# Copying router logits out of PSUM one batch earlier on VectorE, in the opening stage of a two-layer attention and mixture-of-experts kernel

## The chip, the cores and the metric

One core of one Trainium2 chip runs the whole program. The metric is the device time of one execution in microseconds (us), the median of three runs. TensorE is PE in the rows (PEld is its weight load), VectorE is DVE, ScalarE is ACT, GpSimd is POOL, SyncE is SP.

## The reference, cut to what matters

The input x has 8 batches of 512 tokens with 256 features. Layer 0 begins with a layer norm and a small router; the rest of the model (a mixer with cumulative sums, 16 experts that each take 64 tokens of every batch, then attention and 8 experts in layer 1) follows from them and is not touched.

```python
x = L0_attn_x                                   # (8, 512, 256)
xn = _layernorm(x, axis=-1)
s = _L0_attn_ref(xn, ...)                       # mixer
router_logits = jax.nn.silu(xn @ router_w1) @ router_w2      # (8, 512, 16)
expert_probs = jax.nn.softmax(router_logits.transpose(0, 2, 1), axis=-1)
expert_weights, token_indices = jax.lax.top_k(expert_probs, 64)
...
x = x + s * silu(expert output)
```

## The kernel before

The program is a chain of stages, each a block in which every engine works through its own instruction list in order; semaphores tie the lists together, and a block ends when all lists have ended. The stage of this case is the first one after the constants, `layer0_norm`. It loops over the NB = 8 batches; one batch is a tile of 128 partitions with T = 4 tokens each (512 KB). The next stage, `choose_tokens`, ranks tokens on VectorE and needs the logits of all batches.

For batch n the work passes through the engines like this:

- SP loads `x[n]` (`load_x`, L206), two batches ahead at first; in its loop it issues `load_x(n + 2)`, then waits for `xn_done` of batch n and stores `xn` (L217). So `load_x(n + 3)` goes out behind the store of batch n. After the loop it loads `wout` (L218) and writes 8 tiles of zeros to `f` (L220).
- VectorE: `statistics(n)` is four `bn_stats` (L307), four `bn_aggr` (L311) and one add of epsilon (L313). GpSimd raises the result to the power -0.5 (L281). VectorE then does `normalised(n)`, four `tensor_scalar` (L321), the last of which increments `xn_done`.
- TensorE: `transpose_x(n)`, eight 128x128 transposes (L233), waits for `xn_done`. ScalarE copies them to SBUF (L267). `hidden(n)` is the product with router_w1 (L241), ScalarE applies silu (L272), and `logits(n)` is the small product with router_w2 (L249), which increments `lg_ps`.
- VectorE's `logits(n)` waits for `lg_ps` and copies the 128x64 logits from PSUM to `k.logits` (L326), which increments `lg_sb`.

TensorE's list is written in this order: in turn n of its loop it has transposes of batch n + 1, hidden of batch n, logits of batch n - 1:

```python
            for n in range(NB):
                if n + 1 < NB:
                    transpose_x(n + 1)
                hidden(n)
                if n:
                    logits(n - 1)
```

The two PSUM banks for logits are used in turn; TensorE's `logits(n)` waits until VectorE has copied batch n - 2.

VectorE's list in turn n has statistics of batch n + 1, normalised of batch n, and from n = 3 on the copy of batch n - 3; the last three copies stand behind the loop.

Of the kernel before, what the change touches and what calls it, by code (L numbers as in the profile page):

```python
# [14 lines left out]
NB, S, D = 8, 512, 256  # L15
# [32 lines left out]
def land(eng, k):  # L48


    eng.sem_inc(k.made, 1)
# [135 lines left out]
def layer0_norm(nc, R, k, m, x_b, xn_b, f_b, w):  # L187
# [12 lines left out]
    with nc.Block() as block:  # L200

        @block.sync
        def _(sp):
            def load_x(n):
                sp.wait_ge(x_in[n % 2], 16 * (n // 2))
                sp.dma_start(x[n][:], at(x_b, n)).then_inc(x_in[n % 2], 16)  # L206

            load_x(0)
            load_x(1)
            sp.dma_start(rw1[:], w["rw1"]).then_inc(r_in, 16)  # L210
            sp.dma_start(rw2[:], w["rw2"]).then_inc(r_in, 16)
            sp.dma_start(m.wqkv[:], w["wqkv"]).then_inc(m.w_in, 16)
            for n in range(NB):
                if n + 2 < NB:
                    load_x(n + 2)
                sp.wait_ge(xn_done, n + 1)
                sp.dma_start(at(xn_b, n), xn[n % 2][:]).then_inc(xn_out[n % 2], 16)  # L217
            sp.dma_start(m.wout[:], w["wout"]).then_inc(m.w_in, 16)  # L218
            for c in range(NB):
                sp.dma_start(at(f_b, c), k.pad[:, :, 0:D]).then_inc(m.zeroed, 16)  # L220
            for u in range(2):
                sp.wait_ge(xn_out[u], 16 * NB // 2)
# [77 lines left out]
        @block.vector  # L300
        def _(dve):
            def statistics(n):
                dve.wait_ge(x_in[n % 2], 16 * (n // 2 + 1))
                dve.wait_ge(stats_done, 2 * T * n)
                land(nc.vector, k)
                for t in range(T):
                    nc.vector.bn_stats(stats[:, t, :], x[n][:, t, :]).then_inc(stats_done, 1)  # L307
                dve.wait_ge(stats_done, 2 * T * n + T)
                land(nc.vector, k)
                for t in range(T):  # L310
                    nc.vector.bn_aggr(mv[:, n, t, :], stats[:, t, :]).then_inc(stats_done, 1)  # L311
                dve.wait_ge(stats_done, 2 * T * (n + 1))
                nc.vector.tensor_scalar(veps[:, n, :], mv[:, n, :, 1], LN_EPS, None, ALU.add).then_inc(veps_done, 1)  # L313

            def normalised(n):
                dve.wait_ge(rstd_done, n + 1)
                if n >= 2:
                    dve.wait_ge(xn_out[n % 2], 16 * (n // 2))
                    dve.wait_ge(xT_ps, n - 1)
                for t in range(T):  # L320
                    ins = nc.vector.tensor_scalar(xn[n % 2][:, t, :], x[n][:, t, :], mv[:, n, t, 0:1], rstd[:, n, t:t + 1], ALU.subtract, ALU.mult)  # L321
                ins.then_inc(xn_done, 1)

            def logits(n):
                dve.wait_ge(lg_ps, n + 1)
                nc.vector.tensor_copy(k.logits[:, :, n, :], B[6 + n % 2][:, 0:T * E0].rearrange("p (t e) -> p t e", e=E0)).then_inc(lg_sb, 1)  # L326

            statistics(0)
            for n in range(NB):
                if n + 1 < NB:  # L330
                    statistics(n + 1)
                normalised(n)
                if n >= 3:
                    logits(n - 3)
            for n in range(NB - 3, NB):
                logits(n)
            dve.wait_ge(lg_sb, NB)


# [1653 lines left out]
```

## Time and profile before

| | |
|---|---|
| time, median of 3 runs | 1813.77 us (1810.95 to 1816.54) |
| time of the profiled execution | 1813.77 us |
| its span, first to last instruction | 1812.0 us |
| mean granted TensorE clock | 0.930 |
| TensorE busy | 1565.1 us (86%) |
| VectorE busy | 1164.0 us (64%) |
| ScalarE busy | 926.5 us (51%) |
| GpSimd busy | 732.2 us (40%) |

The busy shares are means over all stages. `layer0_norm` runs from 3.66 us to about 51 us of the span. Times of a row count from the start of the span. A row of the time line is: start, length, engine, line, operation, tile written <- tiles read, shape, number of instructions merged in it, and in brackets the idle time of the engine ahead of it and what ended that. The granted clock (PEclk) is a share of full speed: 1.00 is 2.4 GHz and 0.50 is 1.2 GHz.

### The profile page before, as it was taken

How to read it: one execution, taken by the hardware profiler on the slowest of the kernel's cores; microseconds unless marked ns; L12 is line 12 of the kernel's file. 1: busy time of each engine (PE TensorE's matmuls, PEld its weight loads, DVE VectorE, ACT ScalarE, POOL GpSimd, SP SyncE). 2: the span in 40 equal slices, each digit the busy share in tenths (PEclk: the TensorE clock that was granted, in tenths of full speed). 3: DMA queues.
4: the chain of work that ended last, by engine and by line, in shares of the span. 5: the costliest groups of instructions: out<-in, count | busy, mean ns of one | idle time of the engine just before them, and what ended most of it. 6: DMA issues, size and time to landing. Idle time of an engine off the chain costs nothing. (4 is left out here: it accounts for less than half of the span.)

```text
span 1812.0 us, 27053 instructions
## 1 busy us (share of the span) xinstructions
PE 1565.1 (86%) x9562; PEld 1130.2 (62%) x9562; DVE 1164.0 (64%) x1843; ACT 926.5 (51%) x1429; POOL 732.2 (40%) x661
## 2 busy tenths in 40 slices
PE   6279999999999659934999999999999999999871
PEld 4157777777778536622677777777777777777420
DVE  5536756665675356555767666777777777777524
ACT  2144554555455223301555557777767677767442
POOL 4213443363354254503324233555555555555200
PEclk9689999999999868965999999999999999999865
DMA  6524645544342269825233336676767676766435
GB/s 225 164 79 95 167 94 128 135 103 130 70 116 59 34 210 315 311 105 154 83 112 103 112 102 177 173 180 174 187 164 187 165 184 175 189 164 158 81 107 185
DMA packets 218918, 265.38 MB, mean 146 GB/s; under 512 B 19616, under 2 KB 160416, under 8 KB 218784
## 3 DMA queue, kind: packets, MB, share of 16 engines
q1 hardware_dynamic: 191904, 227.92, 41.8%
q0 software_dynamic: 26880, 35.73, 11.1%
q8 instruction: 77, 1.26, 0.3%
q14 instruction: 57, 0.47, 0.1%
HBM read 174.30 MB, written 88.75 MB: 145 GB/s over the span
## 5 line engine op out<-in xcount | busy, mean ns | idle before, releaser
L1603 ACT ACTIVATE a_prob<-a_score_bank 128x1024 f32<-128x1024 f32 x256 | 262.8, 1027 | 288.6 <-PE a_score_bank L1467 250.2
L1718 DVE TENSOR_REDUCE a_neg_max<-a_max_bank 128x2 f32<-128x1024 f32 x256 | 312.8, 1222 | 101.0 <-PE a_max_bank L1450 100.3
L1406 POOL DMA_INDIRECT fs<-a_y,a_token x80 | 127.8, 1598 | 183.5 <-ACT a_y L1644 160.3
L1450 PE MATMUL a_max_bank<-a_ka,a_qa 48*128 48x512 f32 x512 | 133.1, 516 | 46.7 <-DVE a_neg_max L1718 28.7
L1477 PE MATMUL a_bank<-a_prob,a_va 128*32 128x512 f32 x1024 | 145.5, 643 | 0.1
L651 POOL DMA_INDIRECT f<-e_ye,c_slot_row x64 | 100.9, 1577 | 73.8 <-issue 50.0
L1741 DVE SCALAR_TENSOR_TENSOR a_tg<-a_tg,a_bank 128x512 f32<-128x512 f32 x112 | 76.7, 685 | 81.6 <-ACT a_tg L1613 81.6
L1467 PE MATMUL a_score_bank<-a_qa,a_ka 50*128 50x512 f32 x512 | 111.3, 428 | 10.6 <-ACT a_prob L1603 10.5
L1450 PEld LDWEIGHTS a_max_bank<-a_ka,a_qa 48*128 48x128 f32 x512 | 49.5, 190 | 96.6 <-DVE a_neg_max L1718 45.9
L425 PE MATMUL e_bank<-m_wqkv,x_rows 128*128 128x512 f32 (+1 forms) x256 | 93.4, 510 | 14.9 <-DVE e_qkv L679 13.3
L739 DVE TENSOR_TENSOR e_h<-e_bank,e_sge 128x512 f32<-128x512 f32 x64 | 44.3, 692 | 84.2 <-ACT e_sge L563 83.6
L644 POOL DMA_INDIRECT e_xg<-xn,c_slot_row x64 | 71.6, 1119 | 43.7 <-issue 43.7
L93 PE MATMUL a_bank<-a_xThi,late_w31hi 128*128 128x256 f32 x288 | 88.9, 309 | 0.0
L93 PE MATMUL e_bank<-e_w3hi,e_heThi 128*128 128x256 f32 x256 | 81.0, 316 | 7.8 <-DVE e_heTlo L743 7.8
L1613 ACT ACTIVATE a_tg<-a_bank 128x512 f32<-128x512 f32 x112 | 67.2, 600 | 39.2 <-PE a_bank L93 39.0
L1745 DVE TENSOR_TENSOR a_h<-a_bank,a_tg 128x512 f32<-128x512 f32 x112 | 77.5, 692 | 10.7 <-PE a_bank L93 0.4
L93 PE MATMUL a_bank<-a_xThi,late_w11hi 128*128 128x256 f32 x288 | 83.8, 291 | 0.0
L425 PEld LDWEIGHTS e_bank<-m_wqkv,x_rows 128*128 128x128 f32 x256 | 49.3, 198 | 53.0 <-issue 34.8
L93 PE MATMUL a_bank<-a_xTlo,late_w31hi 128*128 128x256 f32 x288 | 81.2, 282 | 0.0
L93 PE MATMUL a_bank<-a_xThi,late_w31lo 128*128 128x256 f32 x288 | 81.2, 282 | 0.0
L93 PE MATMUL a_bank<-a_xThi,late_w11lo 128*128 128x256 f32 x288 | 80.7, 280 | 0.0
L93 PE MATMUL a_bank<-a_xTlo,late_w11hi 128*128 128x256 f32 x288 | 80.7, 280 | 0.0
(330 smaller groups left out, 4701.1 us busy)
## 6 DMA issues: line engine op xcount, KB each, us to landing
late_raw<-in_W SPq DMA_DIRECT2D x120, 512.0 KB, 4.8
e_raw<-in_w SPq DMA_DIRECT2D x48, 512.0 KB, 4.4
a_qa<-qk SPq DMA_DIRECT2D x192, 64.0 KB, 3.9
a_ka<-qk SPq DMA_DIRECT2D x192, 64.0 KB, 3.2
xs<-c_pad SPq DMA_DIRECT2D x20, 516.0 KB, 8.3
a_xg<-xs SPq DMA_DIRECT2D x20, 516.0 KB, 4.6
qk<-p_hi SPq DMA_DIRECT2D x32, 256.0 KB, 5.7
qk<-p_lo SPq DMA_DIRECT2D x32, 256.0 KB, 5.5
```

Source lines behind the costliest of these rows:

```text
L93: ins = nc.tensor.matmul(out, a[i][x], b[l][y], start=first and n == m == 0, stop=last and n == len(pairs) - 1 and m == 2)
L425: ins = nc.tensor.matmul(bank[:, 0:f1 - f0], m.xnT[:, n, ch, t * P:(t + 1) * P], m.wqkv[:, ch, f0:f1], start=ch == 0, stop=ch == DC - 1)
L644: nc.gpsimd.indirect_dma_start(xg[u][:, t, :], None, xn_rows, bass.IndirectOffsetOnAxis(k.slot_row[:, e, t:t + 1], 0)).then_inc(xg_in[u], 16)
L651: nc.gpsimd.indirect_dma_start(f_rows, bass.IndirectOffsetOnAxis(k.slot_row[:, e, t:t + 1], 0), ye[:, t, :], None, compute_op=ALU.add).the ...
L1406: nc.gpsimd.indirect_dma_start(f_rows, bass.IndirectOffsetOnAxis(token[x % 4][:, t:t + 1], 0), y[:, t, :], None, compute_op=ALU.add).then_ ...
L1450: nc.tensor.matmul(M[:, s, :], qa[q][rows, p, t * P:(t + 1) * P], ka[q][rows, p, :], start=True, stop=True).then_inc(p1_ps, 1)
L1467: nc.tensor.matmul(S2[:, s, :], ka[q][rows, p, j * P:(j + 1) * P], qa[q][rows, p, :], start=True, stop=True).then_inc(s_ps, 1)
L1477: ins = nc.tensor.matmul(OB[rows, :], va[g % NR][:, j, rows], prob[j % 2][:, h_, :], start=j == 0, stop=j == T - 1, tile_position=(0, 32 * ...
L1603: nc.scalar.activation(prob[j % 2][:, 2 * p:2 * p + 2, :], S2[:], ACT.Exp, scale=float(D) ** -0.5).then_inc(p_done, 1)
L1718: nc.vector.tensor_reduce(neg_max[:, g % 2, :, T * p + t], M[:], AX.X, ALU.max, negate=True).then_inc(mx_done, 1)
L1741: nc.vector.scalar_tensor_tensor(tg[:], tg[:], 1.0, GATE[:], ALU.add, ALU.mult).then_inc(act_done, 1)
L1745: nc.vector.tensor_tensor(h[:], VALUE[:], tg[:], ALU.mult).then_inc(h_done, 1)
```

## The change

VectorE's copy of the logits comes one turn earlier: behind `normalised(n)` stands the copy of batch n - 2, from n = 2 on, and two copies are left behind the loop. Nothing is added or removed, and no other engine's list is altered.

```diff
                 if n + 1 < NB:
                     statistics(n + 1)
                 normalised(n)
-                if n >= 3:
-                    logits(n - 3)
-            for n in range(NB - 3, NB):
-                logits(n)
+                if n >= 2:
+                    logits(n - 2)
+            logits(NB - 2)
+            logits(NB - 1)
             dve.wait_ge(lg_sb, NB)
```

## Rows read from the trace of the kernel before

**Rows 1.** Waits of VectorE in the stage: total us, times, longest us.

```profile
DVE n_stats L307 <- DMA n_x<-in_x: 11.4, 4, 7.6
DVE c_logits L326 <- PE n_bank L249: 10.2, 6, 3.4
```

**Rows 2.** Time line of VectorE, turns 2 to 5 of the loop.

```profile
20.03 1.38 DVE L321 TENSOR_SCALAR n_xn<-n_x,n_mv,n_rstd 128x256 f32<-128x256 f32 x4
21.42 1.53 DVE L307 BATCH_NORM_STATS2 n_stats<-n_x 128x6 f32<-128x256 f32 x4
...
25.24 0.22 DVE L326 COPY c_logits<-n_bank 128x64 f32<-128x64 f32 x1 [0.23 <-PE n_bank L249]
...
30.25 0.22 DVE L326 COPY c_logits<-n_bank 128x64 f32<-128x64 f32 x1
...
30.38 1.40 DVE L307 BATCH_NORM_STATS2 n_stats<-n_x 128x6 f32<-128x256 f32 x4
...
32.45 1.38 DVE L321 TENSOR_SCALAR n_xn<-n_x,n_mv,n_rstd 128x256 f32<-128x256 f32 x4
```

**Rows 3.** Time line of TensorE in the stage.

```profile
13.22 1.97 PE L233 MATMUL n_bank<-c_ident,n_xn 128*128 128x128 f32 x8 [13.22 <-DVE n_xn L321]
16.65 1.94 PE L233 MATMUL n_bank<-c_ident,n_xn 128*128 128x128 f32 x8 [1.47 <-DVE n_xn L321]
18.39 2.37 PE L241 MATMUL n_bank<-x_rows,n_rw 128*128 128x512 f32 x4
21.47 1.10 PE L233 MATMUL n_bank<-c_ident,n_xn 128*128 128x128 f32 x8 [0.72 <-DVE n_xn L321]
...
24.24 0.96 PE L249 MATMUL n_bank<-n_rw,n_hT 128*128 128x16 f32 x8
...
30.39 1.10 PE L233 MATMUL n_bank<-c_ident,n_xn 128*128 128x128 f32 x8 [1.53 <-DVE n_xn L321]
...
33.04 0.96 PE L249 MATMUL n_bank<-n_rw,n_hT 128*128 128x16 f32 x8
...
42.21 1.07 PE L233 MATMUL n_bank<-c_ident,n_xn 128*128 128x128 f32 x8
```

**Rows 4.** Time line of VectorE, from the copy of turn 6 to the end.

```profile
38.61 0.22 DVE L326 COPY c_logits<-n_bank 128x64 f32<-128x64 f32 x1
...
38.77 1.41 DVE L321 TENSOR_SCALAR n_xn<-n_x,n_mv,n_rstd 128x256 f32<-128x256 f32 x4
...
42.40 0.23 DVE L326 COPY c_logits<-n_bank 128x64 f32<-128x64 f32 x1 [2.22 <-PE n_bank L249]
...
50.65 0.23 DVE L326 COPY c_logits<-n_bank 128x64 f32<-128x64 f32 x1 [0.73 <-PE n_bank L249]
```

**Rows 5.** Time line of SyncE's queue: the last issues of the stage.

```profile
40.61 1.11 SPq L218 DMA_DIRECT2D m_wout<-in_w_out  x1
41.77 9.12 SPq L220 DMA_DIRECT2D f<-c_pad  x8
```

**Rows 6.** Time line of TensorE in the two stages behind.

```profile
51.42 0.63 PE L131 MATMUL ct_bank<-c_ident,c_logits 128*128 128x128 f32 x4 [0.81 <-PEq L200]
...
75.45 5.46 PE L425 MATMUL e_bank<-m_wqkv,x_rows 128*128 128x512 f32 x8 [1.56 <-PEq L122]
...
98.59 2.85 PE L425 MATMUL e_bank<-m_wqkv,x_rows 128*128 128x512 f32 x8 [1.11 <-DVE e_qkv L679]
```

**Rows 7.** Stretches: bounds, length, busy by engine, granted clock, DMA share, GB/s.

```profile
53.50:75.40 21.90, 0.69 (x2) 0.29 (x2) 19.52 (x53) 0.09 (x1) 0.00 (x0) 0.50 0.09 30
75.40:80.70 5.30, 5.25 (x8) 2.53 (x8) 0.07 (x1) 1.06 (x1) 3.74 (x4) 0.50 0.87 234
80.80:84.20 3.40, 0.11 (x1) 0.00 (x0) 1.05 (x1) 0.00 (x0) 2.51 (x3) 1.00 0.97 295
84.20:92.00 7.80, 0.01 (x1) 0.01 (x1) 4.52 (x5) 2.98 (x4) 1.89 (x2) 0.50 0.74 251
92.00:97.80 5.80, 5.48 (x8) 2.48 (x8) 0.29 (x1) 0.88 (x4) 0.00 (x0) 0.50 0.94 280
```

## The prediction

> **What bounds the kernel now.** TensorE is the busiest engine over the whole program, but a share over the whole program says nothing of this change, which touches only the first stage; so I read that stage alone. First the waits of VectorE: in the whole stage it waits 11.4 us for loads of x, of which 7.6 are the start, and 10.2 us for logits [rows 1]. Then the time line, to see where those 10.2 us lie. Inside the loop there is next to nothing: the copy in turn 3 waits 0.23 us, that in turn 4 nothing, and statistics follow at once [rows 2]. The waits for logits are the three copies behind the loop (the first 2.22 us) and cost nothing there, for VectorE has no other work left [rows 4]. Then TensorE: each turn is one burst, transposes, hidden, logits, begun by the end of VectorE's normalised (at 30.39 after 1.53 us idle) [rows 3]. Last, the end of the stage: SyncE issues its zero tiles until 41.77 + 9.12 = 50.89 us, and VectorE's last copy ends at 50.65 + 0.23 = 50.88 [rows 4, 5]. Both hang on the end of normalised(7), at 38.77 + 1.41 = 40.18: SyncE's store and fill by 50.89 - 40.18 = 10.71 us, and TensorE, whose transposes of batch 7 start at 42.21 because it is still in its burst before, by 50.88 - 42.21 = 8.67 us from there.
>
> **What the change does.** It adds no instruction. It moves a wait. In turn n the copy now asks for logits(n - 2). In TensorE's list that product stands behind the transposes of batch n, which wait for the normalised(n) that VectorE has only just finished. So the copy's wait can't be over before a whole burst has run: transposes of n, hidden(n - 1), logits(n - 2). Behind the waiting copy in VectorE's list stand statistics(n + 1) and normalised(n + 1), and for these wait GpSimd's power, SyncE's store and its next load, and TensorE's next burst. Today a burst on TensorE and the statistics on VectorE run side by side; they would run one after the other.
>
> The row shows the length directly: normalised(2) ends at 20.03 + 1.38 = 21.41 [rows 2], and the logits of batch 0 are ready at 24.24 + 0.96 = 25.20 [rows 3]. The copy that stood unblocked one turn later would wait 3.8 us here. There is no deadlock: TensorE's logits(n - 2) needs only the copy of n - 4, two turns back.
>
> **The new turn, with TensorE at full clock.** From the end of normalised to the first transpose 0.06 us (21.41 to 21.47). The burst: 30.39 to 34.00, so 3.61 us [rows 3]. From the end of the logits to the copy 0.04 us (25.20 to 25.24). From the start of the copy to the start of the statistics 0.13 us (30.25 to 30.38), and from there to the end of normalised 32.45 + 1.38 - 30.38 = 3.45 us [rows 2]. Sum 0.06 + 3.61 + 0.04 + 0.13 + 3.45 = 7.29 us for a turn.
>
> Normalised(3) then ends at 25.24 + 0.13 + 3.45 = 28.82, (4) at 36.11, (5) at 43.40, (6) at 50.69. Turn 7 has no statistics: first transpose to copy 0.06 + 3.61 + 0.04 = 3.71, and from the copy to the end of normalised 40.18 - 38.61 = 1.57 [rows 4], so 50.69 + 3.71 + 1.57 = 55.97. That is 15.8 us later than 40.18. The loads of x don't add to it: x4 had landed by 21.42 [rows 2], the later ones are issued behind each store as now, and find 7.3 us between two turns; the waits of the loop for them, 11.4 - 7.6 = 3.8 us in three [rows 1], are all or nearly all swallowed by the new one, and the sum above already counts them as gone from turn 3 on.
>
> **The end of the stage.** SyncE: 55.97 + 10.71 = 66.7. TensorE now stands idle when normalised(7) ends: 55.97 + 0.06 + 8.67 = 64.7. So SyncE's fill ends last, and the stage is 15.8 us longer. If the fill went out quicker on emptier queues, TensorE's 64.7 would bound it: 13.8 us. No work behind the stage covers this: choose_tokens is VectorE's own chain, and it starts when the block ends.
>
> **The clock.** At full clock each burst is followed by 0.04 + 0.13 + 3.45 + 0.06 = 3.68 us without a matmul. How does the granted clock take that? The last transposes of the next stage end at 52.05 [rows 6] and from 53.5 on the clock is 0.50 [rows 7]: it fell within 1.5 us of the last matmul. The burst at 75.45 ends at 80.91, and the clock is 1.00 until 84.2 and 0.50 after it: within 3.3 us. Both are shorter than 3.68, so I take it that each of the four long gaps (ahead of the transposes of batches 3, 4, 5 and 6) costs the clock, and that the burst behind it starts at 1.2 GHz. How long it stays there: the burst from 75.4 ran 5.3 us at 0.50 before the clock rose, the one from 92.0 5.8 us [rows 7]. What half clock costs: the same eight matmuls took 5.46 us at 0.50 and 2.85 at 1.00, 1.92 times as long [rows 6]. So in 5.3 us a burst gets 5.3 / 1.92 = 2.76 us of its 3.61 us of work done and loses 2.54 us; with 5.8 us, 2.78 us. Four bursts: 10.2 to 11.1 us. Normalised(7) ends at 55.97 + 10.2 = 66.2, and ahead of the transposes of batch 7 the gap is only about 1.7 us, like the 1.53 us at 30.39 over which the clock held. SyncE sets the end: 66.2 + 10.7 = 76.9, 26.0 us later than now; at the upper price 26.9.
>
> The profiled execution took 1813.77 us, just the median of the runs, with a span of 1812.0 and 1.8 us around it. 1813.8 + 26.0 to 26.9 gives 1839.8 to 1840.7; I say 1840.
>
> A rule speaks for a worse case. Rows first: at the start, two sets of eight transposes (1.97 and 1.94 us) ran slow, and the hidden product behind them took 2.37 us where at half clock it would take more [rows 3]; so the transposes seem to have counted toward the rise. The Trainium skill, "TensorE: Matmul & The Clock Gate", section "Part 4: PE-mode transpose", says that the full clock does not engage for transposes, since they don't count as busy time in the same way. By that rule every burst, which begins with eight transposes, would run slow to its end, the third rival below; by the row it wouldn't. I go by the row and leave the rule its chance.
>
> **Rivals.**
>
> *The clock holds.* The gap of 3.68 us is close to the 3.3 us over which it once held; the early part of the stage could also carry it. Then the stage is 13.8 to 15.8 us longer: 1827.6 to 1829.6. Against it stands the fall within 1.5 us.
>
> *The clock stays at half from the first gap to the end of the stage.* Each of four bursts loses 3.61 x 0.92 = 3.3 us, normalised(7) ends at 69.3, and TensorE's tail sets the end: 69.3 + 8.7, plus 0.92 times its 7.7 us of work there (transposes, hidden and logits 3.8, hidden 2.0, logits 1.9), is 85.1: 34.2 us longer, 1848. Against it: both restarts of the trace reached 1.00 within 5.8 us [rows 7].
>
> *Not slower.* If logits(n - 2) were ready when the moved copy comes to it, the change would only clear one copy from behind the loop: 0.23 us at most, 1813.6. It decides as soon as the five waits of turns 2 to 6 stay under about 1 us each. For it speaks only that the copies inside the loop hardly wait now; against it the order of TensorE's list, and 3.8 us between the two rows of turn 2.
>
> **How the numbers follow.** Clock lost in each gap 0.61, clock holds 0.22, half clock throughout 0.12, not slower 0.05. A measurement tells about 0.3%, 5.4 us, from no change; all cases but the last are beyond it, so slower 0.95, same 0.04, faster 0.01. The forecast's own range is 1836 to 1843: 2.5 or 2.8 us for each burst, one gap more or less that costs the clock, and the spread of the runs. To hold 8 in 10 it must take in the case in which the clock holds, and leaves out half clock throughout: 1828 to 1845.
>
> **What would show it.** Right: VectorE's copies in turns 2 to 6 each wait 3.7 us or more for TensorE's logits; turns of 7.3 us, or of nearly 10 where the clock fell; normalised(7) ends at about 66 us; granted clock below 1.00 between 29 and 66 us; the fill of zeros ends last, and everything behind the stage is shifted and else unchanged. Wrong: copies in the loop without a wait; an end of normalised(7) near 56 (clock held) or 69 (half clock throughout); or a later stage that gives time back.

## The result, and the profile after

The changed kernel took 1843.56 us (median of 4 runs, 1842.24 to 1847.37), the kernel before 1814.84 us (4 runs): a ratio of 1.0166, 95% interval 1.0146 to 1.0185: slower. The forecast was 1840. The profiled execution has a span of 1843.3 us against 1812.0.

The waits of VectorE in the stage, which answer to [rows 1]:

```profile
DVE c_logits L326 <- PE n_bank L249: 39.8, 8, 6.5
DVE n_stats L307 <- DMA n_x<-in_x: 9.2, 2, 7.7
```

The copies now wait 39.8 us in place of 10.2, all eight of them, and the waits for loads inside the loop have shrunk from 3.8 us in three to 9.2 - 7.7 = 1.5 us in one. The one that is left stands ahead of statistics(3), before the first moved copy, so the change couldn't touch it. The time line of VectorE, against [rows 2]:

```profile
20.13 1.38 DVE L321 TENSOR_SCALAR n_xn<-n_x,n_mv,n_rstd 128x256 f32<-128x256 f32 x4
26.49 0.22 DVE L326 COPY c_logits<-n_bank 128x64 f32<-128x64 f32 x1 [4.98 <-PE n_bank L249]
27.07 1.40 DVE L307 BATCH_NORM_STATS2 n_stats<-n_x 128x6 f32<-128x256 f32 x4 [0.35 <-issue]
...
36.63 0.22 DVE L326 COPY c_logits<-n_bank 128x64 f32<-128x64 f32 x1 [6.10 <-PE n_bank L249]
...
46.60 0.23 DVE L326 COPY c_logits<-n_bank 128x64 f32<-128x64 f32 x1 [6.35 <-PE n_bank L249]
...
56.70 0.23 DVE L326 COPY c_logits<-n_bank 128x64 f32<-128x64 f32 x1 [6.48 <-PE n_bank L249]
...
66.87 0.23 DVE L326 COPY c_logits<-n_bank 128x64 f32<-128x64 f32 x1 [6.55 <-PE n_bank L249]
67.01 1.38 DVE L321 TENSOR_SCALAR n_xn<-n_x,n_mv,n_rstd 128x256 f32<-128x256 f32 x4
```

Every copy waits, and from copy to copy it is 10.1, 10.0, 10.1 and 10.2 us. Normalised(7) ends at 67.01 + 1.38 = 68.39, against 40.18 before. TensorE on its side, against [rows 3]:

```profile
30.59 1.97 PE L233 MATMUL n_bank<-c_ident,n_xn 128*128 128x128 f32 x8 [4.13 <-DVE n_xn L321]
32.35 3.44 PE L241 MATMUL n_bank<-x_rows,n_rw 128*128 128x512 f32 x4
35.63 0.96 PE L249 MATMUL n_bank<-n_rw,n_hT 128*128 128x16 f32 x8
40.31 1.97 PE L233 MATMUL n_bank<-c_ident,n_xn 128*128 128x128 f32 x8 [3.71 <-DVE n_xn L321]
42.06 3.62 PE L241 MATMUL n_bank<-x_rows,n_rw 128*128 128x512 f32 x4
45.48 1.09 PE L249 MATMUL n_bank<-n_rw,n_hT 128*128 128x16 f32 x8
```

The gap ahead of the transposes is 4.13 us the first time and then 3.71 (3.68 was worked out), and the transposes behind it take 1.97 us where they took 1.10, the hidden product 3.62 where it took 1.88. Stretches of the changed kernel, columns as in [rows 7], show why; the granted clock goes 0.50, 1.00, 0.50 and so on:

```profile
28.80:35.40 6.60, 4.81 (x12) 3.12 (x13) 1.70 (x8) 0.00 (x0) 1.29 (x1) 0.50 0.49 159
35.60:38.80 3.20, 0.99 (x9) 0.86 (x7) 1.99 (x10) 1.57 (x3) 0.00 (x0) 1.00 0.00 0
39.00:45.60 6.60, 5.29 (x14) 3.23 (x14) 1.25 (x4) 0.00 (x0) 1.29 (x1) 0.50 0.52 159
45.80:49.00 3.20, 0.77 (x7) 0.67 (x6) 2.22 (x11) 1.50 (x3) 0.03 (x1) 1.00 0.00 0
```

The clock falls in each gap and comes back near the end of the burst, and most of its full stretch is then spent on the next gap (0.99 and 0.77 us of matmuls in 3.2 us). The end of the stage, from the time lines of SyncE's queue, of VectorE and of TensorE, against [rows 4, 5] and the first row of [rows 6]:

```profile
69.36 9.77 SPq L220 DMA_DIRECT2D f<-c_pad  x8
78.18 0.23 DVE L326 COPY c_logits<-n_bank 128x64 f32<-128x64 f32 x1 [0.73 <-PE n_bank L249]
79.67 0.92 PE L131 MATMUL ct_bank<-c_ident,c_logits 128*128 128x128 f32 x4 [1.53 <-PEq L200]
```

SyncE's fill of zeros ends last, at 79.13, VectorE's last copy at 78.41, and the next stage's transposes start at 79.67, 28.25 us later than at 51.42.

### The profile page after: what moved, and what is told of

It is laid out like the page before. It is cut to its first block and busy times, and to the rows that moved or that the text cites. A ratio compares the mean times of both kernels' runs of the same rounds, so it can differ in the third digit from the quotient of the medians.

```text
span 1843.3 us, 27053 instructions
## 1 busy us (share of the span) xinstructions
PE 1582.2 (86%) x9562; PEld 1138.2 (62%) x9562; DVE 1163.3 (63%) x1843; ACT 925.6 (50%) x1429; POOL 729.7 (40%) x661
## 5 line engine op out<-in xcount | busy, mean ns | idle before, releaser
L1467 PE MATMUL a_score_bank<-a_qa,a_ka 50*128 50x512 f32 x512 | 112.5, 433 | 10.2 <-ACT a_prob L1603 10.1
```

Source lines behind the costliest of these rows:

```text
L1467: nc.tensor.matmul(S2[:, s, :], ka[q][rows, p, j * P:(j + 1) * P], qa[q][rows, p, :], start=True, stop=True).then_inc(s_ps, 1)
```

## The experiments

**Fillers in the gaps.** How much of the loss is the wait itself and how much the clock? This run keeps the wait and takes away the idle time.

```diff
                 if n:
                     logits(n - 1)
+                if 1 <= n <= 5:
+                    for _ in range(3):
+                        nc.tensor.matmul(B[2 * (n % 2)][:], rw1[:, 0, :], m.xnT[:, n, 0, :], start=True, stop=True)
             logits(NB - 1)
```

> The changed kernel, with three extra 128x512 matmuls (router_w1 by a finished batch, into a PSUM bank that nobody needs any more; their result is not used) behind the logits of batches 0 to 4 in TensorE's list. They fill most of each 3.7 us gap. My theory (part of the loss is the wait, the other part the clock that falls in each gap): the granted clock stays at 1.00 from the second or third burst on, bursts of 3.6 us, turns of 7.3 us in place of 9.7 to 10.2, normalised(7) ends at 56 to 58 us in place of 68.4, the stage some 11 us shorter than in the changed kernel, time about 1832. Rival (the clock costs nothing, the wait alone does it): no gain, or a loss by the added work, 1843 or more.

Measured: 1833.08 us (5 runs), ratio to the kernel before 1.0093 (1.0076 to 1.0110), against 1.0166 without fillers. TensorE did 15 matmuls more (the profile lists each as two, so three show as x6), and the kernel was faster. Time lines of VectorE and TensorE:

```profile
26.88 0.23 DVE L329 COPY c_logits<-n_bank 128x64 f32<-128x64 f32 x1 [5.47 <-PE n_bank L249]
...
34.61 0.23 DVE L329 COPY c_logits<-n_bank 128x64 f32<-128x64 f32 x1 [3.70 <-PE n_bank L249]
...
41.93 0.23 DVE L329 COPY c_logits<-n_bank 128x64 f32<-128x64 f32 x1 [3.70 <-PE n_bank L249]
...
56.71 1.38 DVE L324 TENSOR_SCALAR n_xn<-n_x,n_mv,n_rstd 128x256 f32<-128x256 f32 x4
```

```profile
34.42 2.82 PE L262 MATMUL n_bank<-x_rows,n_rw 128*128 128x512 f32 x6
38.28 1.09 PE L233 MATMUL n_bank<-c_ident,n_xn 128*128 128x128 f32 x8 [1.04 <-DVE n_xn L324]
39.21 1.88 PE L241 MATMUL n_bank<-x_rows,n_rw 128*128 128x512 f32 x4
40.93 0.96 PE L249 MATMUL n_bank<-n_rw,n_hT 128*128 128x16 f32 x8
```

The stretch that holds all of these turns was granted the full clock:

```profile
21.30:68.80 47.50, 39.66 (x173) 23.31 (x171) 16.12 (x65) 11.62 (x22) 12.11 (x11) 1.00 0.51 169
```

The gap is 1.04 us, all matmuls of the stretch run at the short lengths, and the wait of a copy is 3.70 us, the bare burst (only the first copy waits longer, 5.47 us). A turn is 41.93 - 34.61 = 7.32 us. Normalised(7) ends at 56.71 + 1.38 = 58.09, 10.3 us earlier than in the changed kernel. So the rival that the clock costs nothing is out. The wait costs most all the same: at full clock the kernel is still 18 us slower than the kernel before, which took 1815.00 us beside it.

**TensorE's list in another order.** The wait was put down to where the logits stand in TensorE's list, behind transposes that VectorE has just released. This run keeps VectorE's changed list and alters TensorE's.

```diff
             for n in range(NB):
+                if n:
+                    logits(n - 1)
                 if n + 1 < NB:
                     transpose_x(n + 1)
                 hidden(n)
-                if n:
-                    logits(n - 1)
             logits(NB - 1)
```

> The changed kernel, with TensorE's list altered: logits of batch n - 1 stand ahead of the transposes of batch n + 1 and not behind hidden of batch n. VectorE's list stays as changed. My theory (the wait exists only because the asked-for logits stand behind transposes that VectorE has just released): the copies in the loop wait for next to nothing, turns of 3.6 to 5 us, time 1812 to 1817. TensorE may lose up to 0.9 us a turn where it now waits for silu ahead of the logits. Rival (an earlier copy costs by itself, whatever TensorE's order): 1840 or more.

Measured: 1817.23 us (12 runs), ratio 1.0011 (0.9998 to 1.0024). Of the 28 us at the end of the stage 1.8 are left (the next stage's transposes start at 53.19 us, 51.42 before). They show in the time lines of VectorE and TensorE:

```profile
35.61 0.22 DVE L326 COPY c_logits<-n_bank 128x64 f32<-128x64 f32 x1 [0.77 <-PE n_bank L249]
```

```profile
34.50 1.06 PE L249 MATMUL n_bank<-n_rw,n_hT 128*128 128x16 f32 x8 [0.69 <-ACT n_hT L272]
```

The copies in turns 4 to 6 wait 0.77 us, because TensorE now waits 0.69 us for ScalarE's silu ahead of each logits product. A copy of batch n - 2 is thus not costly by itself, and the rival of 1840 or more is out.

**Two moved copies in place of five.**

```diff
-                if n >= 3:
+                if n in (2, 3):
+                    logits(n - 2)
+                elif n >= 5:
                     logits(n - 3)
```

> The kernel before, with only the copies of batches 0 and 1 one turn earlier (turns 2 and 3, none in turn 4, from turn 5 on as before). My theory (each moved copy costs one burst, and the clock falls in each long gap): normalised(4) ends about 10 us later than the 30.33 of before, the rest keeps that distance, time 1823 to 1826. Rival with the clock at full: 5.8 us later, 1820. Rival in which the loss is not per copy but comes from the copies at the end of the loop: 1814.

Measured: 1824.08 us (6 runs), ratio 1.0040 (1.0025 to 1.0056). The copies of turns 2, 3 and 5 in its time line of VectorE:

```profile
26.38 0.23 DVE L326 COPY c_logits<-n_bank 128x64 f32<-128x64 f32 x1 [4.88 <-PE n_bank L249]
...
36.77 0.23 DVE L326 COPY c_logits<-n_bank 128x64 f32<-128x64 f32 x1 [6.37 <-PE n_bank L249]
...
46.88 0.23 DVE L326 COPY c_logits<-n_bank 128x64 f32<-128x64 f32 x1 [3.12 <-PE n_bank L249]
```

The two moved copies wait 4.88 and 6.37 us, and normalised(4) ends at 39.01 + 1.38 = 40.39, 10.1 us later than before. The copy of turn 5 wasn't moved, but TensorE was still at the slow burst behind the second gap, so that copy waits 3.12 us too. The stage then ends near 62.8 us, 11.9 later than the 50.9 of before; the medians differ by about 9 us (1815.00 for the kernel before), and the ratio says 7 (4.5 to 10). Two moved copies cost less than five, and 5.8 us, the sum at full clock, is too little for this trace, though the ratio alone doesn't rule it out. As a measurement of the price of a copy the time is coarser than the trace.

**A copy one turn later instead.** Batch n - 4 behind normalised(n), from n = 4 on, four copies behind the loop.

```diff
-                if n >= 3:
-                    logits(n - 3)
-            for n in range(NB - 3, NB):
+                if n >= 4:
+                    logits(n - 4)
+            for n in range(NB - 4, NB):
```

> The kernel before, with the copy one turn later: batch n - 4 behind normalised(n), four copies behind the loop. My theory (a copy whose logits are long done costs only its 0.2 us wherever it stands): VectorE's copies in the loop wait for nothing, the stage ends within 0.5 us of before, time within 0.3% of 1814. Rival (more copies behind the loop lengthen the end of the stage): later by up to 1 us, not more, since they wait there for TensorE.

Measured: 1814.78 us (1 run). No copy in the loop waits, and VectorE's last one ends at 51.00, 0.1 us later than before. Distances of 4 and 3 turns are equally good here; the step from 3 to 2 crosses the edge. Longer ones were not run.

**The fill of zeros out of the stage.** The prediction let SyncE's fill set the end. This run is the changed kernel with the fill in the next stage's list.

```diff
-            for c in range(NB):
-                sp.dma_start(at(f_b, c), k.pad[:, :, 0:D]).then_inc(m.zeroed, 16)
...
+        @block.sync
+        def _(sp):
+            for c in range(NB):
+                sp.dma_start(at(f_b, c), k.pad[:, :, 0:D]).then_inc(m.zeroed, 16)
```

> The changed kernel, with SyncE's eight stores of zeros moved into the next stage, choose_tokens, where SyncE has nothing to do. In the changed kernel the fill ends at 79.13 us and VectorE's last copy at 78.41. My theory (the fill ends last, TensorE's tail is less than 1 us behind it): the stage ends 0.7 us earlier, with VectorE's last copy, and nothing else moves; the time stays within the spread of the changed kernel, 1842 to 1847. Rival (the fill takes bandwidth or time from the stage): 2 us or more earlier.

Measured: 1843.34 us (1 run). Normalised(7) ended at 66.10 here, 2.3 us earlier than in the profile after. That is not the fill's doing, for no fill had begun in either kernel. The clock had risen earlier against the work (the first hidden product took 2.51 us, 3.58 in the profile after): the first copy was ready at 25.25 in place of 26.49, and the four bursts behind it were 1.0 us shorter together. Counted from the end of normalised(7), the next stage starts 76.71 - 66.10 = 10.61 us later, against 79.67 - 68.39 = 11.28: 0.67 us gained, and TensorE's tail is right behind. So the next stage starts 3.0 us earlier, as the rival had it, but 2.3 of these are no effect of the fill; by this one execution the fill itself costs 0.7 us.

**Do transposes raise the clock?** The prediction left a chance to the rule that they don't. 40 transposes of the identity stand at the head of TensorE's list, where it would wait for the first load.

```diff
+            for _ in range(40):
+                nc.tensor.transpose(B[7][:, 0:P], k.ident[:], k.ident[:])
             transpose_x(0)
```

> The kernel before, with 40 transposes of the identity into a spare PSUM bank at the head of TensorE's list, while it waits for the first batch (3.7 to 13.2 us); their result is not used. If transposes count for the clock as matmuls do: the granted clock is 1.00 before 13 us, the first two sets of transposes take 1.1 us in place of 1.97 and 1.94. If they don't count: all 40 at half clock, 8.7 us, and the two sets still take 1.9 us or more. The time stays within 1 us of before, since turn 2 waits for its load.

Measured: 1813.28 us (1 run). Time line of TensorE:

```profile
3.71 7.19 PE L253 MATMUL n_bank<-c_ident 128*128 128x128 f32 x40 [3.71 <-PEq L1878]
13.37 1.09 PE L233 MATMUL n_bank<-c_ident,n_xn 128*128 128x128 f32 x8 [2.46 <-DVE n_xn L323]
16.99 1.94 PE L233 MATMUL n_bank<-c_ident,n_xn 128*128 128x128 f32 x8 [2.53 <-DVE n_xn L323]
18.72 3.62 PE L241 MATMUL n_bank<-x_rows,n_rw 128*128 128x512 f32 x4
```

Stretches of the same run:

```profile
3.70:9.00 5.30, 5.29 (x25) 5.30 (x26) 1.23 (x4) 1.25 (x1) 0.10 (x1) 1.00 0.73 246
9.20:15.80 6.60, 2.79 (x24) 2.32 (x22) 5.97 (x29) 1.29 (x3) 2.45 (x3) 1.00 0.70 245
16.00:22.70 6.70, 5.71 (x15) 3.52 (x16) 4.96 (x19) 1.20 (x2) 2.18 (x2) 0.50 0.73 231
```

The first 25 transposes took 5.3 us, the other 15 under 2 us, and the transposes of batch 0 then took 1.09 us where they took 1.97: the clock rose with nothing but transposes run. (The 1.00 of the first row is no reading: the clock's record begins with its first change, near 9.1 us. The length of the transposes tells the level there.) Then, with TensorE idle 2.46 and 2.53 us, it fell before 16, and batch 1 ran slow again.

With 7 matmuls of 128x512 (identity by zeros) in place of the transposes:

> The kernel before, with 7 matmuls of 128x512 (identity by a tile of zeros) at the head of TensorE's list in place of the transposes of the run above; their result is not used. The clock rises before 13 us under either theory about transposes, and the first two sets of transposes take 1.1 us. It shows whether any work at the head does this here, so that the run above can be read.

Measured: 1811.03 us (1 run). The transposes of batches 0 and 1:

```profile
13.11 1.09 PE L233 MATMUL n_bank<-c_ident,n_xn 128*128 128x128 f32 x8 [0.85 <-DVE n_xn L323]
16.53 1.94 PE L233 MATMUL n_bank<-c_ident,n_xn 128*128 128x128 f32 x8 [2.33 <-DVE n_xn L323]
```

Batch 0 ran at full clock, batch 1 again at half. So one expectation failed in both runs, that the transposes of batch 1 would take 1.1 us too: the clock didn't last from batch 0 to batch 1.

**A better version.** The kernel before waits for loads. First the loads alone, one turn earlier:

```diff
+            load_x(2)
             for n in range(NB):
-                if n + 2 < NB:
-                    load_x(n + 2)
+                if n + 3 < NB:
+                    load_x(n + 3)
```

> The kernel before, with each load of x issued one turn earlier (batch 2 ahead of SyncE's loop, batch n + 3 in turn n ahead of the store of batch n). The kernel before waits 3.8 us for loads inside the loop, 1.44 of them ahead of turn 2. My theory: these waits go, VectorE's turns are 3.6 us each, and from turn 3 on TensorE (3.65 us a burst) is as near; normalised(7) and with it SyncE's fill end 2 to 4 us earlier, time 1810 to 1813, at the edge of what can be measured. Rival (the transfers are held by the queues and not by the order of issue): no change of the waits, 1815.

Measured: 1815.23 us (12 runs), ratio 0.9997 (0.9981 to 1.0013). A miss: the waits for loads inside the loop are gone, but normalised(7) ends only 1.4 us earlier, and the time shows nothing. The time line of TensorE, and VectorE's first copy:

```profile
18.36 3.43 PE L242 MATMUL n_bank<-x_rows,n_rw 128*128 128x512 f32 x4
```

```profile
26.27 0.23 DVE L327 COPY c_logits<-n_bank 128x64 f32<-128x64 f32 x1 [3.04 <-PE n_bank L250]
```

The product of batch 0 ran at half clock, and VectorE, now nearly a turn ahead, waited 3.04 us for the logits behind it: the same edge as in the change, reached from the other side. So the loads were joined with 8 zero matmuls at the head of TensorE's list and 2 behind the transposes of batch 0:

> The kernel before, with the loads one turn earlier as in the run e5_loads_ahead, and with extra matmuls of 128x512 (identity by zeros, result not used): 8 at the head of TensorE's list and 2 behind the transposes of batch 0. In e5_loads_ahead the waits for loads were gone but hidden(0) took 3.43 us at half clock and VectorE waited 3.04 us for the first logits. My theory (the clock at half there ate what the loads gave): hidden(0) takes 2.0 us, the transposes of batch 2 start at about 20 in place of 21.6, the stage ends 3 to 4 us earlier than before, time 1811 to 1812, ratio 0.998. Rival (the transfers bound the end of the stage): the fill of zeros still ends at 49 to 50 us, 1814.

Measured: 1810.46 us (12 runs), ratio 0.9971 (0.9954 to 0.9988), faster than the kernel before by 0.3%. The transposes of batch 2 start at 19.88 in place of 21.47, and VectorE's last copy ends at 46.99. Time line of SyncE's queue:

```profile
27.51 10.49 SPq L218 DMA_DIRECT2D xn<-n_xn  x4
38.04 0.51 SPq L219 DMA_DIRECT2D m_wout<-in_w_out  x1
38.59 9.80 SPq L221 DMA_DIRECT2D f<-c_pad  x8
```

The fill still ends at 48.39, 1.4 us behind the last copy, so the rival was half right: the stage gained 2.5 us at its end and not the 3.9 by which VectorE's last copy is earlier. The medians differ by 4.6 us; the trace of the stage accounts for 2.5 of them. It took both edits: the next stage starts 1.2 us earlier than before with the loads alone, and no earlier in the run with 7 matmuls at the head alone (51.77). VectorE also waits 1.17 us ahead of normalised(7) for an earlier store of the normalised x, which frees the buffer that it writes, and SyncE's fill is held back with it.

## Why the prediction was right

- **The time.** It lies 0.6 us above the narrower range of 1836 to 1843 and inside the wide one. The medians differ by 28.7 us where 26.0 to 26.9 were forecast; the other 1 us of the distance to 1840 is the kernel before, whose median was 1814.84 and not 1813.8.
- **The moved wait.** Right. The copies in turns 2 to 6 wait for TensorE, five times, because the product that they ask for stands behind transposes that VectorE has only just released. The other order of TensorE's list removes the loss with the same VectorE list, so this cause is shown, not only argued.
- **A turn of 7.29 us at full clock.** 7.32 us in the run with fillers. The gap of 3.68 us was 3.71 in the changed kernel.
- **The clock falls in each of the four gaps, and each burst loses 2.54 to 2.78 us.** Right. The bursts took 6.00, 6.26, 6.39 and 6.46 us (30.59 to 36.59, and so on), in place of 3.61: 2.4 to 2.9 us each, 10.7 in all against the 10.2 to 11.1 forecast. The fillers, which keep the clock, bring normalised(7) forward by 10.3 us.
- **Half clock throughout.** The sign that the prediction set for this rival, an end of normalised(7) near 69, doesn't tell here: 68.39 lies nearer to the rival's 69.3 than to 66.2. What rules the rival out is the granted clock, which is back at 1.00 at the end of each burst, and the bursts themselves, 6.0 to 6.5 us where half clock to the end would make them 3.61 x 1.92 = 6.9.
- **Normalised(7) at 66.2 us.** It was 68.39. Most of the 2.2 us come from the start: the clock rose at about 21.8 us in this execution and at 19.4 before, so hidden(0) took 3.58 us, and the first copy came at 26.49 where 25.24 had been read off; the first statistics behind it started 0.58 us after the copy began, not 0.13; and the four bursts were 0.5 us longer together. 1.25 + 0.45 + 0.5 is the difference. The 0.58 us is no accident of one execution: in every run with a copy in turn 2 the statistics start 0.56 to 0.58 us behind that copy, and about 0.15 behind the later ones; why stays open. The term "first copy at 25.24" was the mis-sized one: I took it from one execution, though it hangs on when the clock rises against the work, which varies from run to run (25.25 in the run with the fill moved). The sum and the wait were right; a start read from one execution was not safe to 1 us.
- **The clock holds ahead of the transposes of batch 7.** Wrong in its reason. The gap was 1.61 us, about as worked out, but the clock fell at about 69.6, during hidden(6), which took 3.37 us. It made TensorE's tail 10.0 us in place of 8.67 and cost nothing, as SyncE's fill took 10.74 (10.71 forecast).
- **SyncE's fill ends last.** Right, by 0.72 us, and 0.67 us were gained by moving it out.
- **Nothing behind the stage gives time back.** Right. The distance of 28.25 us at the end of the stage is 31.3 at the end of the span; from the next stage's first transposes to the end of the span the profiled executions of this study take 1757.0 (fillers) to 1765.5 us (loads ahead), the kernel before 1760.6 and the changed one 1763.6, so I read nothing into those 3 us.
- **The rule on transposes.** The Trainium skill, "TensorE: Matmul & The Clock Gate", section "Part 4: PE-mode transpose", has it that the full clock does not engage for them. The run with 40 transposes contradicts it for the f32 transposes of this kernel: they alone brought the clock up. Going by the row and not by the rule was right; by the rule the forecast would have been the third rival's 1848.

## What to carry to other kernels

Where two engines work through lists in order, count for each wait what stands ahead of its product in the producer's list: if one of those entries waits for what the waiting engine has just released, the wait costs the producer's whole turn, however small the consumer. Such a hand-over also strips both engines of their overlap and opens gaps on TensorE, and the gaps can cost more than half as much again through the clock: 10.3 us here, on top of the 17.9 by which normalised(7) was late with the clock kept. Removing a wait near such an edge (loads one turn earlier) gave nothing measurable here until the producer was brought along too.

## What I had not expected of the hardware

The granted clock fell over gaps shorter than the 3.7 us of the changed kernel: with TensorE idle 2.46 and 2.53 us on either side of a 1.09 us set of transposes it fell before 16 us, in the run with 7 matmuls at the head it was lost though TensorE idled only 0.85 and 2.33 us around that set, and in the changed kernel it fell behind a gap of 1.61 us that came after a burst run mostly at half clock. It held over 1.53 us in the kernel before [rows 3] and over 1.04 us in the run with fillers. The moment at which it rises in the first stage lay between about 19.4 us (the kernel before) and 22.2 us (the run with two moved copies) in executions whose work up to there was alike. These two are estimates from how long the first hidden product and the transposes behind it took: 2.37 and 1.10 us in the one, 3.62 and 1.33 in the other. Where VectorE waits for the product of batch 0, as in the changed kernel, this matters: normalised(7) ended 2.3 us apart in two executions with the same work up to there. Where it doesn't, as in the run with the copy one turn later (first hidden product 3.30 us), the stage ended within 0.2 us of before.
